# The normalisation of x1 in a gated mLSTM and mixture-of-experts kernel, moved from VectorE to ScalarE, with its transposes placed later on TensorE

## The reference

```python
x = x + tanh(g_xattn) * mlstm(layernorm(x), ctx, ctx, gates, ln_weight)      # x1 from here on
xn = layernorm(x)                                                            # mean and variance over 512 features
gates = softmax(xn @ Wg.T); top 2 experts, with a capacity per expert
out = x + tanh(g_ffn) * sum of the chosen experts' gelu(xn @ W1 + b1) @ W2 + b2
```

## Time and profile before

| | us |
|---|---|
| median of 3 runs | 1995.03 (1991.71 to 1996.44) |
| the profiled execution, its own time | 1997.23 |
| its span, first to last instruction | 1995.2 |
| first part, to the first products of the experts at L879 | 384.0 |
| one slot in the middle of it (slots 3, 4, 5) | 33.0, 33.4, 32.9 |

### The profile page before, as it was taken

The page is one execution under the profiler, slowest core; times in us unless marked ns, Lnnn a source line. Parts: engine busy times, 40 slices in busy tenths (PEclk is TensorE's granted clock), DMA queues, the critical chain, the costliest instruction groups (busy, mean ns, idle before and its releaser), DMA issues.

```text
span 1995.2 us, 28698 instructions
## 1 busy us (share of the span) xinstructions
PE 1899.8 (95%) x10268; PEld 1655.8 (83%) x10268; DVE 752.3 (38%) x1827; ACT 790.7 (40%) x1667; POOL 344.1 (17%) x302
## 2 busy tenths in 40 slices
PE   4999987799999999999999999999999999999997
PEld 3777766688888888888888888888888888888886
DVE  3589987412351235123512351235123512351221
ACT  2567667542352235223522352235223522352221
POOL 0001010262201220122012201220122012201200
PEclk8899987699999999999999999999999999999998
DMA  4255443331241123112311231123212321231111
GB/s 145 85 179 203 163 154 127 96 133 31 64 136 37 31 68 135 34 30 65 134 37 30 62 134 40 30 55 133 48 30 55 132 49 30 57 106 31 31 15 15
DMA packets 111349, 158.10 MB, mean 79 GB/s; under 512 B 13744, under 2 KB 63024, under 8 KB 110208
## 3 DMA queue, kind: packets, MB, share of 16 engines
q1 hardware_dynamic: 92800, 120.68, 18.0%
q0 software_dynamic: 18432, 35.69, 10.2%
HBM read 121.13 MB, written 35.20 MB: 78 GB/s over the span
## 4 chain that ended last, share of the span: by engine, by line
PE 84%; DMA 6%; DVE 4%; issue 3%; ACT 2%; SPq 1%; POOL 0%; POOLq 0%; DVEq 0%; ACTq 0%
PE PS L892 38%; PE PS L879 36%; DMA out_dram<-y_out,rows_add 3%; PE PS L731 3%; PE PS L722 2%; DMA vs<-in_ctx_dram 2%; PE PS L862 2%; PE PS L670 1%; PE PS L750 1%; ACT heads L976 1%; SPq L420 1%; DVE stats L1178 1%; PE PS L684 1%; DMA gathered<-xn_rows,rows_turn 1%; DVE decay L1236 0%
## 5 line engine op out<-in xcount | busy, mean ns | idle before, releaser
L1135 ACT ACTIVATE h_raw<-PS,b_now 128x360 f32<-128x360 f32 x384 | 215.5, 561 | 1035.9 <-PE PS L879 1033.9
L1495 DVE TENSOR_TENSOR h_lo<-h_raw,h_hi 128x360 fp32r<-128x360 f32 x384 | 205.2, 534 | 1074.5 <-ACT h_hi L1136 1073.6
L879 PE MATMUL PS<-x_hi,w_hi 128*128 128x360 f32 x1536 | 503.6, 328 | 2.7 <-issue 1.4
L879 PE MATMUL PS<-x_hi,w_lo 128*128 128x360 f32 x1536 | 503.5, 328 | 0.0
L879 PE MATMUL PS<-x_lo,w_hi 128*128 128x360 f32 x1536 | 501.9, 327 | 0.0
L892 PE MATMUL PS<-w_hi,h_hi 128*120 128x512 f32 x1152 | 459.9, 399 | 0.0
L892 PE MATMUL PS<-w_lo,h_hi 128*120 128x512 f32 x1152 | 453.9, 394 | 0.0
L892 PE MATMUL PS<-w_hi,h_lo 128*120 128x512 f32 x1152 | 453.2, 393 | 0.0
L603 POOL DMA_INDIRECT out_dram<-y_out,rows_add x72 | 129.1, 1793 | 1197.5 <-DVE y_out L1523 986.1
L879 PEld LDWEIGHTS PS<-x_hi,w_hi 128*128 128x128 f32 x1536 | 289.8, 189 | 25.0 <-issue 3.9
L879 PEld LDWEIGHTS PS<-x_lo,w_hi 128*128 128x128 f32 x1536 | 289.3, 188 | 16.4
(11 more groups left out here) (177 smaller groups left out, 1432.5 us busy)
## 6 DMA issues: line engine op xcount, KB each, us to landing
raw<-in_L_ffn_W_dram SPq DMA_DIRECT2D x128, 512.0 KB, 4.5
x_front<-in_x_dram SPq DMA_DIRECT2D x8, 1024.0 KB, 7.1
vs<-in_ctx_dram SPq DMA_DIRECT2D x32, 256.0 KB, 4.7
maxima<-maxima_rows SPq DMA_DIRECT2D x8, 1024.0 KB, 4.7
x_back<-in_x_dram SPq DMA_DIRECT2D x8, 1024.0 KB, 8.9
out_dram<-x_back SPq DMA_DIRECT2D x8, 1024.0 KB, 6.9
xn_rows<-xn SPq DMA_DIRECT2D x8, 1024.0 KB, 9.5
b_row<-in_L_ffn_b_dram SPq DMA_DIRECT2D x8, 256.0 KB, 3.6
```

What stands on the lines that cost most here:

```text
L879: ins = T.matmul(PS[:, HB + n % 3, 0:CW], w[:, w_at(j), k * P:(k + 1) * P], v[:, c, k, :], start=(k == 0 and a == 0), stop=(k == KT - 1 an ...
L1135: A.activation(h_raw[:, n % 3, :], PS[:, HB + n % 3, 0:CW], ACT.Gelu, bias=b1_now[:, n % HT:n % HT + 1])
L1495: V.tensor_tensor(h_lo[:, n % 3, :], h_raw[:, n % 3, :], h_hi[:, n % 3, :].bitcast(F32), ALU.subtract)\
```

## The change

VectorE's `second_norm` no longer writes xn. After the Newton steps it waits until the normalisations of the batch before are made (a signal that is one slot old) and makes the bias, minus mean times inverse deviation, in one small instruction for all four tiles. ScalarE gets `normalise_x1(last, t)`: xn of tile t as Identity of x1 times the inverse deviation plus the bias, the form that the last batch had already. It runs in the slot after the one in which VectorE did it before. The four stand between the copies of the front tiles: one behind `copy_front` 3, one behind 4, two behind 5, and the first `copy_back`, which stood ahead of all of these, follows the fourth. After the fourth, ScalarE waits for its own four results and signals `xn_made`, which lets SyncE store xn. On TensorE the four `turn_back` each wait for their own tile's signal, not for all of xn, and the first two are placed later. For batch 6 the four normalisations stand after ScalarE's slot 7, ahead of the copies. The last batch does what it did.

```diff
@@ TensorE, turn_back
-                if in_slot(b, B - 1):
-                    pe.wait_ge(last_normed, t + 1)
-                else:
-                    pe.wait_ge(xn_made, START + at(b, 1, 1))
+                pe.wait_ge(x1_normed, at(b, 4, t + 1))
@@ TensorE, slot
                 when(front, turn_front, 3)
-                when(last, turn_back, 0, spread)
                 when(front, turn_front, 4)
                 when(front, turn_front, 5)
+                when(last, turn_back, 0, spread)
+                when(front, turn_front, 6)
                 when(last, turn_back, 1, spread)
-                when(front, turn_front, 6)
                 when(front, turn_front, 7)
                 when(last, turn_back, 2, spread)
                 when(b, outputs, 0)
@@ ScalarE
+            def normalise_x1(b, t):
+                p = b[1] % 2
+                if t == 0:
+                    act.wait_ge(x1_scaled, at(b, 1, 1))
+                    act.wait_ge(back_turned, START + at(b, 4, 0))
+                    act.wait_ge(xn_stored, at(b, 16, 16))
+                A.activation(xn[:, t, :], x_back[p][:, t, :], ACT.Identity, bias=small[2][:, 5, t:t + 1],
+                             scale=small[2][:, 3, t:t + 1]).then_inc(x1_normed, 1)
+                if t == ST - 1:
+                    act.wait_ge(x1_normed, at(b, 4, ST))
+                    act.sem_inc(xn_made, 1)
@@ ScalarE, slot
+                when(front, copy_front, 3)
+                when(last, normalise_x1, 0)
+                when(front, copy_front, 4)
+                when(last, normalise_x1, 1)
+                when(front, copy_front, 5)
+                when(last, normalise_x1, 2)
+                when(last, normalise_x1, 3)
                 when(last, copy_back, 0, False)
-                when(front, copy_front, 3)
-                when(front, copy_front, 4)
-                when(front, copy_front, 5)
+                when(front, copy_front, 6)
                 when(last, copy_back, 1, False)
-                when(front, copy_front, 6)
                 when(front, copy_front, 7)
                 when(last, copy_back, 2, False)
@@ ScalarE, behind slot 7
+            for t in range(ST):
+                normalise_x1(near(LAST_BATCH, -1), t)
             act.wait_ge(head_summed, NH * B)
@@ VectorE, second_norm
-                dve.wait_ge(back_turned, START + at(b, 4, 0))
-                dve.wait_ge(xn_stored, at(b, 16, 16))
-                for t in range(ST):
-                    ins = normalise(2, t, xn, x_back[b[1] % 2])
-                ins.then_inc(xn_made, 1)
+                wait_past(dve, x1_normed, at(b, 4, 0))
+                V.scalar_tensor_tensor(small[2][:, 5, 0:ST], small[2][:, 0, 0:ST], -1.0, small[2][:, 3, 0:ST],
+                                       ALU.mult, ALU.mult).then_inc(x1_scaled, 1)
```

More of the change, by code:

```diff
@@ L257, in build @@
         x1_scaled = sem("x1_scaled")
-        last_normed = sem("last_normed")
+        x1_normed = sem("x1_normed")
         onehot_used = sem("onehot_used")
@@ L1088, in _ @@
             seed(2, LAST_BATCH, fixed)
-            def normalise_last(t):
-                A.activation(xn[:, t, :], x_back[LAST_BATCH[1] % 2][:, t, :], ACT.Identity, bias=small[2][:, 5, t:t + 1],
-                             scale=small[2][:, 3, t:t + 1]).then_inc(last_normed, 1)
-            act.wait_ge(x1_scaled, 1)
-            act.wait_ge(back_turned, START + at(LAST_BATCH, 4, 0))
-            act.wait_ge(xn_stored, at(LAST_BATCH, 16, 16))
-            normalise_last(0)
-            normalise_last(1)
+            normalise_x1(LAST_BATCH, 0)
+            normalise_x1(LAST_BATCH, 1)
             copy_back(LAST_BATCH, 0, True)
-            normalise_last(2)
+            normalise_x1(LAST_BATCH, 2)
             copy_back(LAST_BATCH, 1, True)
-            normalise_last(3)
+            normalise_x1(LAST_BATCH, 3)
             copy_back(LAST_BATCH, 2, True)
             copy_back(LAST_BATCH, 3, True)
-            act.wait_ge(last_normed, ST)
-            act.sem_inc(xn_made, 1)
             copy_router(LAST_BATCH)
@@ L1437, in _ @@
             second_stats(LAST_BATCH, link)
-            newton(2, LAST_BATCH, ST, link)
-            V.scalar_tensor_tensor(small[2][:, 5, 0:ST], small[2][:, 0, 0:ST], -1.0, small[2][:, 3, 0:ST],
-                                   ALU.mult, ALU.mult).then_inc(x1_scaled, 1)
+            second_norm(LAST_BATCH, link)
             select(1, link)
```

## The result

The changed kernel takes **2023.2 us** (median of 4 runs, 2021.34 to 2027.59) against 1995.74 for the kernel before on the same chip: 1.0143 times as long, with a 95% interval of 1.0119 to 1.0167. 2021.4 was forecast, with a range of 2010 to 2031. The profiled execution took 2021.34 us with a span of 2019.4, which is 24.2 more than the span before.

| | before | after |
|---|---|---|
| first product of the experts | 384.0 | 407.6 |
| from there to the end of the span | 1611.2 | 1611.8 |
| slot 2, scores of head 0 to the next slot's | 37.3 | 40.0 |
| slot 3 | 33.1 | 40.0 |
| slot 4 | 33.4 | 37.9 |

The account below looks back on a forecast made before the run. It took the context loads' landing, with TensorE full behind it, to bound the slots. Slots 3 to 5 18.0, slot 2 3.3, slot 6 4.4, slot 7 1.2, end -0.5: 26.4 on 1995.03, so 2021.4 us, range 2010 to 2031.

Parts of the forecast that it names:

- The picture: Each slot: 7.4 us from issue of context loads to landing, then 25.6 us of full TensorE; time added behind landing lengthens it.
- VectorE's relief: The 1.7 us that VectorE saves per slot was costed at nothing in slots 3 to 6.
- ScalarE's chain at full clock: Behind the landing, normalisations delay the first xn copy; outputs start 6.4 us after landing instead of 2.8, 3.6 later.
- The clock: Slots 3 to 5: 1.2 GHz from about the landing, back within the outputs, making such a slot cost 6.0 us.
- The small slots: Separate terms for slot 2 (3.3 us), slot 6 (4.4 us) and slot 7 (1.2 us).
- The end: Last batch: its heads start at 327.1 instead of 327.64, a term of -0.5 us.
- The sum: Whole kernel: the slot terms and the end add 26.4 us to the median, giving 2021.4 us.
- that the clock holds: Rival: no clock fall in slots 3 to 6, adding 18.0 us, so 2013 us; chance 0.17.
- VectorE's queue: Rival: VectorE's queue sets the slot, so relieving it makes the kernel faster by 10.7 us, 1984 us; chance 0.05.
- that the copies keep pace: Rival: second xn transpose needn't wait for the first copy, adding only 2.5 us, so 1997.5 us; chance 0.05.
- that the low clock lasts beyond the outputs: Rival: 7.3 us in each of slots 3 to 6 and 4.5 in slot 2, so 2029 us; chance 0.08.

Follow-up runs that it names:

- e7: Kernel before, with the context loaded by head instead of by tile, three of four loads issued at the end of the previous slot: 1992.9 us.
- e10: Kernel before, with VectorE writing only 64 of the 512 columns of xn and ScalarE given nothing: 1993.9 us, ratio 0.9987.
- e4: Changed kernel with the third and fourth normalisation moved behind the first xn copy on ScalarE: 2009.5 us.
- e3: Changed kernel with two unused filler products in each of TensorE's two waits (before context, before second xn tile) of slots 2 to 6: 2037.2 us.
- e12: Changed kernel with two filler products in each of TensorE's two waits of slots 2 to 6 and one more in slot 1: 2013.6 us.
- e1: Kernel before, VectorE still writing xn, with only TensorE's transposes and ScalarE's copies in the changed order: 2003.3 us, ratio 1.0035.
- e9: Changed kernel with filler products in slots 2 to 6, two ahead of the context and three in the wait for the copy: 2011.3 us.

## Why the prediction was right, step by step

**The picture** (end of a slot, landing, full TensorE): right for the step that decides, in that every us added behind the landing showed in the slot. The landing ends last in slots 2 to 5 of the kernel before and of e7 alike. What would bound a slot without it shows in slot 6 of e7 alone: VectorE's xn and ScalarE's copies, close behind. It did no harm, as in e10 an earlier xn only made the wait for the landing longer.

**VectorE's relief, costed at nothing**: right. e10 takes half of it for no one's loss and gains 0.13%, in an interval that holds 1. The wait for the logits stayed at 1.18 us (1.20 in the earlier trace rows). The few tenths that the landing might gain are not shown: it came 7.02 us behind its issue instead of 7.43 in slot 4, but 8.38 instead of 7.13 in slot 3, and over slots 2 to 6 it took 2.0 us more in sum (37.7 against 35.7). In the runs that load by tile that sum goes from 34.8 (e4) to 38.5 (e3) without an order that follows the changes.

**ScalarE's chain at full clock**: right to a quarter of a us. Outputs at 6.4 behind the landing were worked out; 6.50 to 6.64 were measured in e12 in slots 3 to 6. The first copy stood at 4.04 instead of 3.98, and the wait for its own last result, put at 0.2 without a row, took 0.17.

**The clock**: right that it falls, wrong in where. The wait ahead of the landing was taken to be 2.5 us; it was 3.34, 2.08 and 2.15 in slots 3 to 5. The clock was taken to fall from the landing on in slots 3 to 5 and to be back within the outputs. It did so in slots 3 and 5, and in slot 3 it was back while TensorE waited for the copy and fell again. In slots 4 and 6 it fell only behind that wait, with the last three of the seven groups of transposes to go. So the transposes lost less than the 1.35 us that separates 7.75 from 6.4, and from the outputs' start to the next scores it took 0.25 to 1.0 us longer than before, not 1.05 in each. A slot cost 4.5 to 5.0 us instead of 6.0 (slots 4 and 5); slot 3 cost 6.9, of which 1.25 come from a landing that was later in this run. Together slots 3 to 5 cost 16.4 against 18.0. That these sums come so near is in part luck, since the low clock lay elsewhere than it was priced. In all the prediction adds 8.4 us for it (26.4 against 18.0 if it holds); e12 shows 5.0 by the stretch and 9.3 by the ratios.

**The small slots**: slot 2 cost 2.7 (3.3 forecast), slot 6 cost 5.1 (4.4: it fell behind the second wait as slot 4 did), slot 7 cost 0.1 (1.2). In slot 7 the chain was right and the clock was not (TensorE, for the earlier trace rows):

```profile
313.22 1.12 PE L747 MATMUL PS<-ident,xn 128*128 128x128 f32 x4 [6.50 <-ACT xn L963]
316.18 1.09 PE L747 MATMUL PS<-ident,xn 128*128 128x128 f32 x4 [1.84 <-ACT xnT L955]
318.03 1.09 PE L747 MATMUL PS<-ident,xn 128*128 128x128 f32 x4 [0.77 <-ACT xnT L955]
318.91 3.29 PE L731 MATMUL PS<-vs,decay 128*128 128x129 f32 x20
```

The outputs start 5.69 us behind the first xn tile instead of 4.62, but they take 3.29 instead of 4.51, since the clock came back earlier. **The end**: the heads of the last batch start 24.46 us later (352.10 against 327.64 in the earlier trace rows), where slot 7 had stood at 24.99: -0.5, as forecast. Up to the experts another 0.8 went, which the sum did not have.

**The sum**: 26.4 forecast, 24.2 by the spans, 27.5 by the medians. Errors of both signs cancel in it: slots 2 to 5 and 7 were put 3.3 too high, slot 6 was put 0.7 too low, and 2.0 of what the slots cost come from later landings, which no term had. It splits along the runs: places 3.8, normalisations in the copies' way 13.1 (e1 to e12, both at full clock in slots 3 to 6), clock 5.0 (e12 to after) by the stretch, and 7.0, 12.2 and 9.3 by the ratios. The split by the ratios is rough: e9, whose waits are filled too, lies 6 us below e12 by its ratio, which would give the clock 15.8 and the normalisations 5.8. The rivals: that the clock holds was priced at 2013, and e12, where it is made to hold, takes 2013.6 (e9 2011.3); VectorE's queue (1984) falls by e10; that the copies keep pace (1997.5) falls by the wait of 2.69 us; that the low clock lasts beyond the outputs (2029) was nowhere seen in slots 3 to 6 (its 7.3 us a slot don't come out of its terms either: 4.95 and 2.1 make 7.05).

## What to carry to other kernels

Ask not how long a moved instruction takes on its new engine but what is queued behind it there, and who waits for that: the same 1.4 us a slot cost 9 us in front of a copy that frees a bank and nothing in the idle time some us earlier. Give a waiting bank's copy the first place in its engine's order, and test a relief by itself (do half of the work, for no one) before paying for it elsewhere. Where short waits lie on both sides of a little matrix work, look at the granted clock before and behind the second wait too. And when a view names what ended a wait, check that it ended before the work began.

## What the runs showed of the hardware

- The place of code, as far as e3, e9 and e12 show, can cost nearly as much as the change under study: e3 and e12 differ by one matrix product in slot 1 and by 23.6 us in the medians. In the profiles 16.2 us of it lie in the experts, where e3 has a standstill of TensorE of 2.6 to 3.2 us in each of the six turns of a loop that neither kernel touches.
- The clock does not fall behind every wait of a given length: 2.08 us ahead of the landing in slot 4 of the changed kernel left it at 1.00, 2.15 in slot 5 was followed by 0.50 at 236, 2.22 in slot 3 of e1 left it at 1.00 again, and in slot 3 of the changed kernel it was back just as the work stopped and stayed up through a us without any (161.0 to 162.0). The Trainium skill ("TensorE: Matmul & The Clock Gate", HAM oscillation) tells of a kernel that its waits between bursts of matrix work set back to the low clock every time. Here some waits did it and others of about the same length did not, and what makes the difference is open.
- ScalarE's wait for its own last result took 0.17 us, once a slot.
